# First sparse layer of a fused transformer block moved out of the block loop, into a stage of eight token groups with the attention's output projection

## The reference, cut to what matters

```
x = x + attention_a(layernorm(x))    # per batch row; 16 heads of 16; only 307 of the 512 queries of a head are kept
x = x + sparse(layernorm(x))         # the FIRST sparse layer
x = x + attention_b(layernorm(x))    # rmsnorm, gated linear attention over the 8 rows as time, wo, then rmsnorm + gated ffn
x = x + sparse(layernorm(x))         # the second sparse layer, same weights

def sparse(x):                       # w1: 1024 x 256, w2: 256 x 1024, 16 blocks of 64 hidden channels
    mask = top 4 of the 16 logits x @ router_w.T + router_b
    h = relu(where(mask, x @ w1.T + b1, 0))
    return h @ w2.T + b2
```

## Time and profile before

| what | us |
|---|---|
| median of 3 runs | 1966.01 (1960.99 to 1967.28) |
| the profiled execution itself | 1954.64 |
| its span, first to last instruction | 1952.9 |
| attention, to the last signal of its units | 0 to 602.8 |
| project | 602.8 to 670.6 |
| block 0 of stream 0 alone, to the first gate product | 670.6 to 808.4 |
| 7 merged iterations, counted from gate product to gate product | 808.4 to 1863.3 |
| block 7 of stream 1 alone | 1863.3 to 1952.9 |

### The profile page before, as it was taken

One profiled execution on the slowest core, in us unless ns is written; L12 is line 12 of the kernel. 1 busy time (PEld: TensorE's weight loads), 2 busy tenths in 40 slices (PEclk: granted clock), 3 DMA queues, 4 the chain that ended last, 5 costly groups with the idle time before them and its releaser, 6 DMA issues.

```text
span 1952.9 us, 26057 instructions
## 1 busy us (share of the span) xinstructions
PE 1569.6 (80%) x8605; PEld 1078.2 (55%) x8660; DVE 1179.1 (60%) x2289; ACT 716.4 (37%) x956; POOL 709.5 (36%) x845
## 2 busy tenths in 40 slices
PE   4789889888965467598798798788788798788876
PEld 2333333333424454476676576676676577577665
DVE  4778777877779725526726726726726726825731
ACT  1366666666662122123223233323333233233212
POOL 5343435333404522234334333333333333333332
...
DMA packets 51831, 56.43 MB, mean 29 GB/s; under 512 B 15296, under 2 KB 37072, under 8 KB 51792
## 3 DMA queue, kind: packets, MB, share of 16 engines
...
...
## 4 chain that ended last, share of the span: by engine, by line
PE 43%; DVE 21%; issue 15%; POOL 9%; ACT 5%; DMA 3%; another core or an unknown queue 2%; SPq 0%; DVEq 0%; POOLq 0%; ACTq 0%
PE ps L1478 13%; PE ps L1502 7%; PE ps L694 5%; POOL h L1140 5%; PE ps L667 4%; PE ps L681 3%; PE ps L628 3%; DVE oT_b L1301 2%; DVE mc L386 2%; PE ps L636 2%; POOL rstd_b L1107 2%; DVE hf L1299 2%; ACT pT0a L560 1%; PE ps L1563 1%
## 5 line engine op out<-in xcount | busy, mean ns | idle before, releaser
L1140 POOL TENSOR_TENSOR h<-hf,h 128x512 fp32r<-128x512 f32 x192 | 260.7, 1358 | 564.8 <-ACT h L1417 386.4
L386 DVE TENSOR_REDUCE mc<-ps 128x2 f32<-128x1024 f32 x256 | 306.7, 1220 | 47.6 <-PE ps L667 47.3
L1502 PE MATMUL ps<-w,h 128*128 128x256 f32 x1536 | 222.5, 293 | 25.4 <-POOL h L1140 24.4
L205 POOL DMA_DIRECT2D k_st<-k_hi x256 | 123.0, 486 | 297.3 <-PE ps L681 279.8
L1478 PE MATMUL ps<-xT_b,w 128*128 128x512 f32 x768 | 220.1, 425 | 6.1 <-ACT maskT L1407 6.1
L1502 PEld LDWEIGHTS ps<-w,h 128*128 128x128 f32 x1536 | 196.3, 190 | 38.8 <-POOL h L1140 34.0
L1365 DVE TENSOR_TENSOR hf<-ps,hf 128x512 f32<-128x512 f32 x64 | 44.2, 690 | 274.0 <-PE ps L1478 272.3
L1414 ACT ACTIVATE hf<-ps,b 128x512 f32<-128x512 f32 x128 | 88.0, 687 | 293.0 <-PE ps L1533 162.4
L667 PE MATMUL ps<-k_st,q_st 48*128 48x512 f32 x512 | 139.4, 542 | 35.7 <-DVE mc L386 33.6
L1478 PEld LDWEIGHTS ps<-xT_b,w 128*128 128x128 f32 x768 | 145.9, 199 | 39.6 <-ACT maskT L1407 9.1
L667 PEld LDWEIGHTS ps<-k_st,q_st 48*128 48x128 f32 x512 | 52.7, 202 | 168.2 <-issue 88.5
...
## 6 DMA issues: line engine op xcount, KB each, us to landing
q_st<-q_hi SPq DMA_DIRECT2D x256, 32.0 KB, 2.0
k_st<-k_hi POOLq DMA_DIRECT2D x256, 32.0 KB, 2.0
x_in<-in_x_dram SPq DMA_DIRECT2D x9, 512.0 KB, 4.3
q_st<-q_lo SPq DMA_DIRECT2D x128, 32.0 KB, 2.2
k_st<-k_lo POOLq DMA_DIRECT2D x128, 32.0 KB, 2.0
x_dram<-x_in SPq DMA_DIRECT2D x8, 512.0 KB, 3.0
x<-x_dram SPq DMA_DIRECT2D x16, 256.0 KB, 3.7
out_dram<-tok SPq DMA_DIRECT2D x16, 256.0 KB, 3.3
```

The lines of the kernel that those rows point to most:

```text
L205: eng.dma_start((q_st, k_st)[which][par][64 * e + DH * r:64 * e + DH * r + DH, j, :].bitcast(F32), src[(2 * j + e) * DH:(2 * j + e + 1) * ...
L386: v.tensor_reduce(mc[par][:, qt, 2 * HU + j:MC:NPAIR], ps[:, at:at + 2, :], AX_X, ALU.max).then_inc(max_done, 1)
L1140: g.tensor_tensor(lo[:, :], hf[s][m % 2][:, :], hi[:, :].bitcast(F32), ALU.subtract).then_inc(S["hl"], 1)
L1502: last = t_.matmul(ps[:, ACC[s] + t // 2, (t % 2) * D:(t % 2 + 1) * D], h[s][m % 2][a][:, t * P:(t + 1) * P], ws[k][:, m, :], start=m == 0 ...
```

## The change

The first sparse layer leaves the block loop. `project` becomes empty (it only waits). In its place `block_part` starts with a stage of eight groups. A group is 128 positions of 4 rows (512 tokens); groups alternate between slot 0 and slot 1 (the two streams' tiles and banks). For each group: `p.mask` (DVE masks `oa`; POOL adds bo to x), `p.T`, `p.wo`, `p.x` (DVE adds the product to x), and the whole sparse layer `f.*`; the result is stored to DRAM as `x1` and read back by blocks as before. The projection and router chain of group n+1 (`chain`) is merged by hand into the hidden products of group n (`hidden`), at the places in `FILL`. The start of block 0 (`z.ln` to `z.T`) is merged into the last group. `MERGED` has no f0 parts any more and its other parts are interleaved anew, with the f1 router parts now among the recurrence steps. `selT` and `oa` are the same; the tiles in SBUF are laid out anew.

The weights w1, w2 and the router's are loaded by SP at the very start of the kernel, copied by ACT before its first `m_copy`, and split by POOL after its first stackings; POOL also makes `expand` there. The other weights are loaded by SP at the start of the new stage and split by ACT and POOL inside groups 0 to 4 and 7 (`LATE_IN`), two pieces behind `f.m2` (three in group 7). The piecewise loads of ACT in `weights_act` are gone.

The core of the diff, the schedule:

```diff
-STREAM0 = ["f0.ln", "f0.T", "f0.rt", "f0.lg", "f0.mk", *steps("f0.m", 8), "f0.end", "z.ln", "z.rms", "z.T",
-           *steps("z.o", NOUT), *steps("rec", T8), "og", "o.mean", "o.ln", "o.T", "o.wo", "o.rms", "o.x"]
...
-MERGED = ["g.T", "g.m0", "g.u0", "f0.ln", "g.m1", "g.u1", "g.d0", "f0.T", "g.m2", "g.u2", "g.d1", "f0.rt",
...
-          "f1.d6", "o.rms", "f1.end", "o.x"]
+NGROUP = 8
+FIRST = NGROUP // 2
+def chain(s):
+    return [f"p{s}.mask", f"p{s}.T", f"p{s}.wo", f"p{s}.x", *(f"f{s}.{k}" for k in ("ln", "T", "rt", "lg", "mk"))]
+def hidden(s, k="f"):
+    return [f"{k}{s}.m0", *(f"{k}{s}.{p}{m - (p == 'd')}" for m in range(1, 8) for p in "md"), f"{k}{s}.d7",
+            f"{k}{s}.end"]
+def merged(a, b, places):
+    out, n = [], 0
+    for k, name in enumerate(a):
+        while n < len(b) and places[n] <= k:
+            out.append(b[n])
+            n += 1
+        out.append(name)
+    return out + b[n:]
+Z_START = ["z.ready", "z.ln", "z.rms", "z.T"]
+Z_REST = [*steps("z.o", NOUT), *steps("rec", T8), "og", "o.mean", "o.ln", "o.T", "o.wo", "o.rms", "o.x"]
+FILL = [0, 2, 4, 5, 6, 9, 11, 13, 15]
+LATE_IN = {0: (0, 1), 1: (2, 3), 2: (4, 5), 3: (6, 7), 4: (8, 9), 7: (10, 11, 12)}
+BEFORE = [(name, 0) for name in ["init", *chain(0)]]
+for _n in range(NGROUP):
+    _s = _n % 2
+    _other = chain(1 - _s) if _n + 1 < NGROUP else Z_START
+    for _name in merged(hidden(_s), _other, FILL if _n + 1 < NGROUP else [5, 8, 11, 14]):
+        BEFORE.append((_name, 0 if _name[0] == "z" else (_n + 1) // 2 if _name in _other else _n // 2))
...
+        if _name == f"f{_s}.m2":
+            BEFORE += [(f"wt{k}", 0) for k in LATE_IN.get(_n, ())]
+BEFORE += [(name, 0) for name in Z_REST]
+MERGED = ["g.T", "g.m0", "g.u0", "z.ln", "g.m1", "g.u1", "g.d0", "g.m2", "g.u2", "g.d1", "z.rms",
+          "g.m3", "g.u3", "g.d2", "g.m4", "z.T", "g.u4", "g.d3", "z.o0", "z.o1", "g.m5", "g.u5", "g.d4", "z.o2",
+          "z.o3", "g.m6", "g.u6", "g.d5", "z.o4", "z.o5", "g.m7", "g.u7", "g.d6", "z.o6", "z.o7", "z.o8",
+          "rec0", "g.d7", "rec1", "g.end", "f1.ln", "rec2", "f1.T", "rec3", "f1.rt", "f1.lg", "rec4", "f1.mk",
+          "f1.m0", "rec5", "f1.m1", "f1.d0", "rec6", "f1.m2", "f1.d1", "rec7", "f1.m3", "f1.d2",
+          "og", "o.mean", "f1.m4", "f1.d3", "o.ln", "f1.m5", "f1.d4", "f1.m6", "o.T", "f1.d5", "o.wo", "f1.m7",
+          "f1.d6", "o.rms", "f1.d7", "f1.end", "o.x"]
```

SP and POOL in the new stage:

```diff
     def sp(eng):
...
+        load_group(0)
+        load_group(1)
+        for out, in_ in small:
+            ld(out, in_, small_in)
+        for src, _, _, raw in late[:NLATE]:
+            ld(raw, src, late_raw)
+        for n in range(NGROUP):
+            s, k = n % 2, n // 2
+            eng.wait_ge(proj[s]["x2"], k + 1)
+            ld(dram["x1_tiles"][:, group(n)[2], :], x[s][:, :, :], x2_out[s])
+            if n + 2 < NGROUP:
+                eng.wait_ge(x2_out[s], 16 * (k + 1))
+                load_group(n + 2)
+            if n == NGROUP - 2:
+                eng.wait_ge(pads_cleared, 1)
+                for src, _, _, raw in late[NLATE:]:
+                    ld(raw, src, last_raw)
+                eng.wait_ge(x2_out[0], 16 * FIRST)
+                eng.wait_ge(x2_out[1], 16)
+                load(0)
...
     def pool(eng):
...
+        def late_low(n):
+            _, hi, lo, raw = late[n]
+            eng.wait_ge(late_hi, n + 1)
+            g.tensor_tensor(lo, raw, hi.bitcast(F32), ALU.subtract).then_inc(late_lo, 1)
+        def bias(k, s):
+            eng.wait_ge(x1_in[s], 16 * (k + 1))
+            g.tensor_tensor(x[s][:, :, :], x[s][:, :, :], bo_all[:, :].unsqueeze(1).to_broadcast([P, NT, D]),
+                            ALU.add).then_inc(proj[s]["biased"], 1)
         def ffn_ln(i, s):
             std(s, F[s], i)
-            eng.wait_ge(F[s]["src"], i + 1)
+            eng.wait_ge(T[s]["src"], turn(i, 1) + 1)
             g.tensor_tensor(x[s][:, :, :], x[s][:, :, :], b2_all[:, :].unsqueeze(1).to_broadcast([P, NT, D]),
                             ALU.add).then_inc(F[s]["biased"], 1)
...
+            parts[f"p{s}.mask"] = lambda k, s=s: bias(k, s)
```

In the attention (`w1`, `w2`, `rw` are `ffn_pieces`, five of them):

```diff
     def sp(eng):
...
+        eng.wait_ge(ffn_cleared, 1)
+        for src, _, raw in ffn_pieces:
+            ld(raw, src, ffn_raw)
...
     def pool(eng):
...
+        for n, (_, ws, raw) in enumerate(ffn_pieces):
+            eng.wait_ge(ffn_hi, n + 1)
+            g_.tensor_tensor(ws[1], raw, ws[0].bitcast(F32), ALU.subtract).then_inc(ffn_lo, 1)
+        g_.memset(expand[:, :], OFF).then_inc(expand_made, 1)
...
     def act(eng):
...
+        eng.wait_ge(ffn_raw, 16 * len(ffn_pieces))
+        for _, ws, raw in ffn_pieces:
+            a.activation(ws[0], raw, ACT.Copy).then_inc(ffn_hi, 1)
         m_copy(0, TASKS_FIRST.index("mx"))
```

More of the change, by code:

```diff
@@ L32 @@
 QUAD = 32
-BELOW_WEIGHTS = 7 * 1024
+BELOW_OUTPUTS = 2900
 O_ROWS = (HG - 1) * QUAD + OR
@@ L136, in attention @@
     rstd = sb("rstd", [P, NT], F32)
-    stage = [oa[:, NC * n:NC * (n + 1), :] for n in range(3)]
-    w_o = [sb(f"wo_a{i}", [P, NC, D], F32R) for i in range(2)]
     bq = sb("bq", [P, NC], F32)
@@ L142, in attention @@
     bv_all = sb("bv_all", [P, D], F32)
+    head_of = sb("head_of", [P, HU], F32)
+    sb("below_outputs", [P, BELOW_OUTPUTS], F32)
+    oa = sb("oa", [P, B * NT, D], F32)
+    selT = sb("selT", [P, NT, P], F32)
+    w_o = [sb(f"wo_a{i}", [P, NC, D], F32R) for i in range(2)]
     bo_all = sb("bo_all", [P, D], F32)
-    head_of = sb("head_of", [P, HU], F32)
+    stage = [oa[:, NC * n:NC * (n + 1), :] for n in range(3)]
     ident, minus_half = const["ident"], const["minus_half"]
@@ new lines, in merged @@
+def merged(a, b, places):
[8 more added lines that the diff above has]
+Z_REST = [*steps("z.o", NOUT), *steps("rec", T8), "og", "o.mean", "o.ln", "o.T", "o.wo", "o.rms", "o.x"]
+W_STREAM = ["g.T", "g.m0", "g.u0", *(f"g.{k}{m - (k == 'd')}" for m in range(1, 8) for k in "mud"), "g.d7", "g.end",
+            "f1.ln", "f1.T", "f1.rt", "f1.lg", "f1.mk", *hidden(1)]
@@ new lines, in block_part @@
+    W = {n: split_home(nc, sb, f"{n}_b", [P, NC, HID] if n != "w_down" else [P, NM, D])
+         for n in ("w_gate", "w_up", "w_down")}
+    W |= {n: split_home(nc, sb, f"{n}_b", [P, NC, D]) for n in ("wk", "wq", "wv", "wog")}
+    y = sb("y", [P, NT, D], F32)
+    qT, kT, vT = (sb(n, [P, NC, L], F32) for n in ("qT", "kT", "vT"))
+    oT = sb("oT_b", [P, NC, L], F32)
+    aT = sb("aT", [P, NC, L], F32)
+    pr = [sb(f"pr{c}", [P, L], F32) for c in range(NC)]
+    gT = two("gT", [P, L])
+    W["wo"] = split_home(nc, sb, "wo_b", [P, NC, D])
@@ new lines, in block_part @@
+    for name in ("w_gate", "w_up"):
+        (hi, lo), raw = W[name]
+        for c in range(NC):
+            late.append((dram[name][c * P:(c + 1) * P, :], hi[:, c, :], lo[:, c, :], raw[:, c, :]))
+    for k in range(2):
+        part = slice(k * NM // 2, (k + 1) * NM // 2)
+        late.append((dram["w_down"][k * NM // 2 * P:(k + 1) * NM // 2 * P, :].rearrange("(m p) n -> p m n", p=P),
+                     *(t[:, part, :] for t in (*w_down, W["w_down"][1]))))
+    NLATE = len(late)
+    whole("wo")
@@ L1040, in weights_act @@
         eng.wait_ge(*const["units_done"])
-        for n in range(len(stage)):
-            fetch(n)
-        for out, in_ in small:
-            eng.dma_start(out, in_).then_inc(small_in, 16)
-        eng.wait_ge(w_cleared, 1)
-        for n, (_, _, ws) in enumerate(pieces):
-            eng.wait_ge(stage_in[n % len(stage)], 16 * (n // len(stage) + 1))
-            nc.scalar.activation(ws[0], staged(n), ACT.Copy).then_inc(stage_hi, 1)
-            if n and n - 1 + len(stage) < len(pieces):
-                eng.wait_ge(stage_lo, n)
-                fetch(n - 1 + len(stage))
```

501 lines of the change are left out of this document (251 added, 250 removed), and 5 rows, old and new, of the table MERGED.

## The result

| | before | after |
|---|---|---|
| median of 4 runs | 1963.5 us | 2078.3 us |
| lowest and highest | 1958.1, 1967.3 | 2075.9, 2081.0 |
| profiled span | 1952.9 | 2079.2 |

The ratio is 1.0622, 95% interval 1.0579 to 1.0664: the change makes the kernel **6.2% slower**. I had forecast slower, but by 1.5% (1995.6 us, range 1945 to 2032). The direction held, the size was wrong by more than the range allowed.

A forecast was written before the change was run, and what follows sets the result against it. Merged iterations were taken as nearly PE-bound, projection and block 0 alone as bound by chains of short steps. 234 us more before the loop less 204.4 saved in it gave 1995.6 us on the median; range 1945 to 2032.

The forecast's parts named there:

- A merged iteration: Block loop: walking the new order engine by engine gives 121.0 us an iteration, 29.2 saved; seven take 850.5.
- recurrence of 43.4 us: In a merged iteration: 27.3 of links and small steps, 9.6 of moved DVE work, and listed waits, 43.4 us.
- one term of 1.5 for the iteration: Merged iteration: 1.5 us of clock cost for two PE waits of 2.5 and a recurrence only 60% busy.
- Rival 3: Loop: the recurrence falls to half clock; 127 an iteration, 42 us more, 2038 in all; chance 0.10.
- From the recurrence's end to g.m0: Last part of a merged iteration, up to the next g.m0: same parts as before, 27.1 us.
- The group period: New stage, groups 1 to 6: 34.4 us undisturbed, 8.0 of wait and 2.0 of cold clock each.
- the late weights: New stage, groups 2 to 4: splits on POOL push the layer norm's power back, 1.5 us three times, 4.5.
- rival 2: New stage: the load's wait is hidden, the six groups cost 60 us less, 1936 in all; chance 0.05.
- The start: Kernel start: loading, copying and splitting five weight pieces costs 0 us, or 5 if the cover is gone.
- The cover I named: Kernel start: DVE's maxima of the first 16 score tiles run during POOL's splits, so the cost is 0.
- From g.m0 to rec0: First part of a merged iteration: 47.5 us to the end of z.o8, then 1.5 for sigmoid and its table load.
- the tail: After the seven iterations: unchanged, 89.6 us.

The follow-up runs named there:

- the collision at the square gone: Changed kernel plus a wait: in the loop POOL's low_h of m4 waits until DVE has squared tok; 2051.9 us, ratio 1.0494 to the kernel before.
- the 12 and 12 times: Merged order and bo addition edits on the changed kernel, timed 12 times without and 12 with POOL's weight subtractions moved behind its last unit: 1967.0 and 1960.9 us.

## Why the prediction was wrong, point by point

- **The step that failed** is "A merged iteration", its recurrence of 43.4 us. The mechanism was the one named, down to the list of waits; their sizes were not: 14.8 to 15.5 instead of 6.5. Half of it is that I walked the recurrence at full clock and put all the clock's cost into one term of 1.5 for the iteration. The clock alone is worth 3 to 4.6 there. The other half are waits that I had too short at any clock. The seven recurrences took 362.0 us instead of 303.8: 58 of the 81 us. The rest is 25 from the recurrence's end to g.m0 and 8 from g.m0 to rec0, less the 10.5 of my clock term.
- **Rival 3** (half clock in the recurrence) was the right direction. I bounded it at 127 by half clock for PE's own pieces. A piece at half clock delays DVE, and with DVE's next product PE again, as I read the timeline; and the clock's fall came on top of longer waits, not in place of them. With the collision at the square gone the iteration is 129.6, which is the number to hold against the 127. I gave it 0.10 and let only half of it into the range. That it had been seen at 0.66 in block 0 alone deserved more.
- **From the recurrence's end to g.m0**, 27.1 "same parts": the parts were the same, the start order of two of them was not, and that cost 3.6 in each iteration, 25 us in all. No row of before showed a price for it, but the earlier trace rows had the hint: low_h had a mean of 1367 ns there, which mixes 22 of 1.26 to 1.40 with two long ones, 2.21 and 2.29.
- **The group period**: 44.4 predicted, 44.4 to 45.2 measured, with the wait of 8.0 before w2 as foreseen (7.98). From the attention's end to the first iteration it was 439.6 predicted, 444.7 measured, and that is closer than its parts: group 7, with `z.ready`, took 40.7, 7.1 more than I gave it, while groups 1 to 6 took 267.9 instead of 270.9, since the late weights (4.5 in my sum) cost nothing there.
- **The price of that wait** in rival 2, 60 us, was too high: 37, since the late weights surface behind it. I had them at 1.5 a group; they cost 4.5 to 5.0 once nothing hides them, and were hidden by the very wait.
- **The start** was costed at 0, with 5 if the cover goes. The cover I named was over when three quarters of the subtractions' time were still to come, and a small step that I hadn't looked at took the loss, about 6 us by the 12 and 12 times. The attention's end was 9.9 later than predicted; what isn't the step is within what it varies from profile to profile.
- **From g.m0 to rec0** (49.0 against 49.9 to 51.1) was nearly right and **the tail** (89.6 against 90.0) right.
- **Two sums** in the prediction are a little off and change nothing: the VectorE work moved into the recurrence adds up to 9.5, not 9.6, and the upper end of the forecast's own range, by its terms, is 2026 and not 2020.
